# Sharing out 32 weight-quantizing units over four attention tiles: 10, 9, 7, 6 instead of 6, 9, 9, 8

## The reference

```
# layer 0
xn = layernorm(x)
scores = (xn Wq^T)(xn Wk^T)^T / sqrt(1024)
scores *= exp(log(decay[s]) * (s - t - 1)) for s > t, else 0      # decay = sigmoid(xn Wd^T + bd)
x = x + (scores @ (xn Wv^T)) Wo^T * out_scale
      + xn @ int4(kernel) + bias + (xn @ a) @ b
# layer 1
xn = layernorm(x)
x = x + exp(log_alpha) * (linear attention with decay gamma, causal) @ W_read^T
      + relu(xn @ tern(W1)^T + b1) @ tern(W2)^T + b2
tern(W) = clip(round(W / (mean|W| + 1e-5)), -1, 1)
```

## Time and profile before

| | us |
|---|---|
| median of the two timed runs (1548.93 and 1549.86) | 1549.39 |
| profiled execution, device time | 1544.3 |
| its span, first to last instruction, on its slowest core (core 4) | 1542.8 |
| spans of the eight cores | 1518.6 to 1542.8 |
| TensorE busy, share of the span | 1225.9, 79% |
| layer-0 attention stage on core 4 | 374.9 to about 759 |

### The profile page before, as it was taken

One profiled execution on the slowest core, in us unless ns is written; L12 is line 12 of the kernel. 1 busy time (PEld: TensorE's weight loads), 2 busy tenths in 40 slices (PEclk: granted clock), 3 DMA queues, 4 the chain that ended last, 5 costly groups with the idle time before them and its releaser, 6 DMA issues. The chain is left out here.

```text
span 1542.8 us, 15297 instructions; the slowest of 8 cores (1518.6 to 1542.8 us)
## 1 busy us (share of the span) xinstructions
PE 1225.9 (79%) x5332; PEld 532.1 (34%) x5440; DVE 418.4 (27%) x704; ACT 474.2 (31%) x550; POOL 137.9 (9%) x184
## 2 busy tenths in 40 slices
PE   0176179996798686683639999999997999999997
PEld 0022034442343232231214444444443444444443
DVE  0498346001323333333247400030002200041000
ACT  0565023334532644627213342014202140032400
POOL 2341100000110210212110000000000000000000
PEclk9999679998899788896969999999998999999999
DMA  8696863002334645757494352354235152252432
GB/s 200 101 166 117 116 102 55 1 1 82 110 102 157 189 139 196 228 165 232 148 157 89 134 141 84 134 191 137 84 135 191 29 154 88 85 191 71 121 110 109
DMA packets 74202, 194.42 MB, mean 126 GB/s; under 512 B 8272, under 2 KB 16496, under 8 KB 69776
## 3 DMA queue, kind: packets, MB, share of 16 engines
q0 software_dynamic: 37072, 105.34, 28.3%
q1 hardware_dynamic: 37056, 88.09, 18.3%
HBM read 195.57 MB, written 33.56 MB: 149 GB/s over the span
## 5 line engine op out<-in xcount | busy, mean ns | idle before, releaser
L1214 PE MATMUL pb<-bigA,wqA 128*128 128x512 bf16 x1002 | 224.7, 379 | 1.2
L1174 PE MATMUL pb<-xn,xbf 128*128 128x512 bf16 x1004 | 221.5, 380 | 1.1
L1157 PE MATMUL pb<-stm,bigB 128*128 128x512 bf16 x627 | 147.7, 394 | 46.3 <-DVE xa_bf L1012 30.1
L1101 ACT ACTIVATE bigA<-pb,cstF 128x512 bf16<-128x512 f32 x128 | 99.5, 777 | 218.0 <-PE pb L1174 218.0
L1196 PE MATMUL pb<-rt,projW 128*128 128x512 bf16 x501 | 125.0, 391 | 41.0 <-DVE rt L1017 36.0
L1047 DVE SCALAR_TENSOR_TENSOR xf<-pb,cstF,xf 128x512 f32<-128x512 f32 x32 | 24.0, 750 | 479.5 <-PE pb L1214 479.5
L1174 PEld LDWEIGHTS pb<-xn,xbf 128*128 128x128 bf16 x1024 | 100.2, 98 | 121.7
L1214 PEld LDWEIGHTS pb<-bigA,wqA 128*128 128x128 bf16 x1024 | 100.2, 98 | 120.8
L1157 PEld LDWEIGHTS pb<-stm,bigB 128*128 128x128 bf16 x640 | 63.5, 101 | 130.2 <-issue 62.2
L429 PE MATMUL pb<-rt,cstB 128*128 128x512 bf16 x110 | 32.2, 418 | 85.9 <-DVE rt L395 85.7
L1089 ACT ACTIVATE statsT<-xbf,cstF 128x1024 bf16<-128x1024 f32 x42 | 52.1, 1240 | 110.3 <-DMA xbf<-W2T 79.1
(11 more groups left out here) (129 smaller groups left out, 1109.2 us busy)
## 6 DMA issues: line engine op xcount, KB each, us to landing
wqA<-W2qS POOLq DMA_DIRECT2D x32, 1024.0 KB, 5.1
xbf<-W1qS SPq DMA_DIRECT2D x128, 256.0 KB, 2.6
xbf<-W2T SPq DMA_DIRECT2D x26, 512.0 KB, 4.1
bigA<-W2T POOLq DMA_DIRECT2D x32, 256.0 KB, 9.0
bigA<-W1T POOLq DMA_DIRECT2D x16, 512.0 KB, 9.8
xf<-xT SPq DMA_DIRECT2D x4, 2048.0 KB, 8.3
x1S<-xf POOLq DMA_DIRECT2D x4, 2048.0 KB, 8.4
stm<-W1T SPq DMA_DIRECT2D x16, 512.0 KB, 5.2
```

The lines of the kernel that those rows point to most:

```text
L1101: got = si(s.activation(bigA[:, fc * 512:(fc + 1) * 512], pb[fc % 2][:, :], AF.Relu, bias=biasL[:, 48 + fc:49 + fc], scale=sc[:, C_Q4:C_Q4 ...
L1157: got = ti(t.matmul(bank[:, :], bigB[:, i * 1024 + ec * 128: i * 1024 + (ec + 1) * 128], stm[:, i * 512:(i + 1) * 512], start=(n == 0), st ...
L1174: got = ti(t.matmul(bank[:, :], xbf[:, (fc % 4) * 1024 + dc * 128: (fc % 4) * 1024 + (dc + 1) * 128], xn[:, p0:p0 + TS], start=(dc == 0), ...
L1214: got = ti(t.matmul(bank[:, :], wqA[:, (dc % 2) * 4096 + fc * 128: (dc % 2) * 4096 + (fc + 1) * 128], bigA[:, fc * 512:(fc + 1) * 512], st ...
```

## The change

One line. Tile 0 quantizes units 0 to 9 (before: 0 to 5), tile 1 units 10 to 18 (6 to 14), tile 2 units 19 to 25 (15 to 23), tile 3 units 26 to 31 (24 to 31). The places of the halves among the anchors follow from the planner's formula, since `NH` changes in tiles 0, 2 and 3. `NSL` is not changed.

```diff
@@ -798,7 +798,7 @@
             prefA.append(v0 + tot)
         totalA = tot
         if layer == 0:
-            QUC = [6, 9, 9, 8]
+            QUC = [10, 9, 7, 6]
             u0 = sum(QUC[:j])
             units_j = list(range(u0, u0 + QUC[j]))
             NH = 2 * len(units_j)
```

## The result

The changed kernel takes 1.0039 times the time of the one before (95% interval 1.0029 to 1.0050, many runs of both on the same chips): 4.5 to 7.7 us more, 6.0 by the ratio. That is slower by less than 2%. The medians are 1554.6 and 1547.4 us; they take in those executions of either kernel in which part of the chip ran slower, and the ratio doesn't.

What follows compares the result with a forecast made beforehand. Layer 0's TensorE waits for VectorE anchors standing behind halves; tile 0's halves are bound by its two slots' turn. Tile 0 +28.4, tile 2 -9.3, tile 3 -10.6 give +8.5 us: 1557.9 us, range 1547 to 1571.

Steps and rivals of the forecast that it cites:

- Ranks: Last halves ahead of anchors by the planner's formula: tile 0 q8 (xa), q14 (R7); R7 in tile 2 q8, tile 3 q5.
- Tile 0's delay: Tile 0's residual phase, behind q14 and R7, starts at 472.5 and not 446.1: 26.4 us late.
- the turn: Tile 0's two slots: one use of a slot, Sign start to the Sign two halves later, takes 11.6 us; seven to q14.
- rival A: Tile 0's two slots: a turn shorter than 10.4 us makes the kernel faster; 1546 at 9.9 us; chance 0.07.
- One reading: Tile 0, kernel before: Sign passes of a slot come 10.7 to 12.9 us apart (2.47 plus 8.2 to 10.4).
- The clock: Tile 0's residual phase starts at TensorE's lower clock after 6 us of idleness: 2.0 us more, between 1.3 and 2.8.
- Tile 1: Tile 1 keeps its number of halves, slots and anchors, so its length doesn't change; W1T's halves make no difference.
- Tiles 2 and 3: R7 hangs on q8, not q11, in tile 2 (9.3 us gained) and on q5, not q8, in tile 3 (10.6 gained).
- The sum: Whole kernel: 28.4 - 9.3 - 10.6 = +8.5 us, on the median 1549.4 giving 1557.9.
- B: Tile 0's extra halves are hidden, bandwidth being the limit, and the gains of tiles 2 and 3 stand: 1529.5; chance 0.03.
- C: R7 in tiles 2 and 3 is held by something else, so only tile 0's cost remains: 1577.8; chance 0.04.
- D: Tile 0's slot turn lengthens under load to 14.8 us, cost 51 us, slower by 2%; chance 0.03.

Runs made afterwards that it cites:

- late_only: Kernel before with its own units; in tiles 2 and 3 the halves stand later among the anchors, q8 and q5 ahead of R7; ratio 0.9893.
- q8987: Kernel before with half the move, units per tile 8, 9, 8, 7, nothing else changed; ratio 0.9989.
- cost_only: Kernel before with four more units in tile 0 and none taken from tiles 2 and 3 (10, 9, 9, 8); ratio 1.0153.
- free_slot: Changed kernel, but in tile 0 sums overwrite the first Sign result, so load slots free after the second Sign pass; ratio 0.9889 to the kernel before.
- early_only: Kernel before, but layer 0's first loads of halves are issued ahead of the x1S store wait and xf load; ratio 0.9879.
- late_early: Kernel before with tile 0's slots freed early, halves placed by due time, early first loads and units 9, 9, 8, 6; ratio 0.9563, 1480.2 us.

## Why the prediction was right

**Ranks.** q8 ahead of xa and q14 ahead of R7 in tile 0, q8 in tile 2, q5 in tile 3: shown in the timeline above; late_only and q8987 show that the rank is what counts.

**Tile 0's delay.** 26.4 us to the residual start was worked out, 23.4 measured (19.4 in the score phase, 4.0 in R). The term that was mis-sized is the turn: 11.63 us, measured 11.2 on core 5 and 11.0 to 11.4 on the others. On the mean of the cores seven turns make -2.5 us, q0's add, 11.75 us into the tile and not 11.1, +0.6; another -1.1 is the baseline, since core 4's residual phase of before starts 67.6 us into the tile and the mean of the eight cores is 68.7. The error in the turn was in the mean over all ten pairs: the chain from q0 to q14 consists of even halves only, whose five pairs of before have a mean of 8.9 us (the odd ones 9.4), and which took 8.8 after. 2.47 + 8.8 is about the 11.2 measured. The direction of rival A was right, its size was far from the 10.4 us at which it decides. The landings stayed at 3.9 us for a load and 3.3 for a store; the estimate beside rival A took the figure for a GpSimd-issued DMA for the load too, which SP issues.

One reading was wrong without harm. The prediction says that the Sign passes of a slot come 10.7 to 12.9 us apart in the kernel before, by adding 2.47 to the add-to-Sign times. In that trace only q2 to q5 are added 2.47 us after their Sign pass (the others stand behind anchors and take 4.7 to 7.9 us), and the passes are 10.9 to 17.3 us apart. In the changed kernel 2.47 holds for nearly all, and they are 10.9 to 12.2 us apart on core 5 after the first two (13.5 and 14.2).

**The clock.** 2.0 us for the lower clock in the residual phase; 1.9 measured, and absent in q8987, whose residual phase has no long idle time ahead of it.

**Tile 1.** 0 predicted, 0.6 measured. W1T's halves made no difference that shows.

**Tiles 2 and 3.** 9.3 and 10.6 predicted, 8.8 and 9.6 measured. The mechanism held, but the sizes come from one core, and in tile 2 that was luck. From q8's add to q11's the kernel before takes 9.3 us on core 4 and 10.6 on the mean of the eight cores; q8 itself then came 1.5 us later into the tile (37.8, 36.4 before), and the residual phase starts 9.1 us sooner. In tile 3 the residual start is 2.2 us behind q5, as worked out, and R7 behind q5 and not q8 is worth 11.3 us on core 4, the most of all cores (mean 9.5), less R6's 0.7; q5 came 0.5 us sooner into the tile (35.0, 35.5 before), and the residual phase starts 9.4 us sooner.

**The sum.** +8.5 predicted, +7.8 in the stage, +6.0 in the timed ratio. The sum is closer than its terms, since the cost was put 3.0 us too high and the gains 1.5. Why the timed runs show 1.8 us less than the stage isn't traced; in cost_only and q8987 it is 2 to 3 us less as well. Rivals B and C are refuted by cost_only and late_only, D by the turn.

What the prediction didn't see is how much lay beside it. It named the two slots as a likely shortage, but took the chain as given and read tile 0's cost as the price of moving units; free_slot shows that most of this price is one wait (a load for a store that used the same buffer), and early_only that another wait of this kind sat ahead of tiles 1 and 3.

## What to carry to other kernels

Where side work is woven into an engine's ordered list, a stage's cost isn't set by how much of it the stage has, but by which piece stands ahead of the anchor that the main engine waits for and when its chain delivers that piece: count ranks and turns, and balance by them, not by the length of the main work. Balancing toward an idle stretch pays only if the chain there has the buffers to go faster: moving units to tile 0 cost 6 us net with two slots held through load, compute and store, and a like move (9, 9, 8, 6) gained 22 with slots freed after their last read, halves placed by due time and first loads issued early. Before moving work, look for the wait that makes its turn long, and for first loads that queue behind a store they don't need.

## What was not expected of the hardware

Loads and stores of halves overlapped well: with both in flight the turn from q0 to q14 fell from 11.2 us to 8.5 on core 0 (7.2 at the shortest shown), on cores that all did the same at once.

TensorE's lower clock doesn't follow only a long idle time right ahead. In late_early's tile 3 on core 1 the granted clock is 1.00 until 641.0 and 0.50 from 641.5, after dense score matmuls and 2.19 us of idleness. It is back at 1.00 by 646, falls again during the 3.81 us of idleness ahead of 652.86, and stays at 0.50 up to 660, so that the residual phase's first 8 matmuls take 3.57 us after only 1.37 us of idleness. The length of the idle time alone doesn't decide it either: on core 6, 3.06 us at the same place as the 2.19 left the first 27 R matmuls as fast as elsewhere (6.20 us; on core 1, 28 took 7.87). In tile 0 of the same execution on core 1 the residual's first 8 take 1.89 after 1.01, behind 27.8 us of dense matmuls.
